# Two deformable convolutions on one core: the last unit's sampling products in two passes by rows of taps, and each pair's output finished in thirds on three engines

## The reference

```python
def gather(yi, xi): ...          # x at a whole pixel, 0 outside
val = gather(y0, x0) * (1-ly)*(1-lx) + gather(y0, x0+1) * (1-ly)*lx \
    + gather(y0+1, x0) * ly*(1-lx) + gather(y0+1, x0+1) * ly*lx      # per tap, at (y + ky - 1 + dy, x + kx - 1 + dx)
val = val * mask                                                     # second block only
out = einsum('bckhw,ock->bohw', val, w) + b
# block 1: x = x + out;  block 2: x = x + relu(norm1(out) * gamma + beta), norm1 over all of an image
```

## Time and profile before

| | us |
|---|---|
| median of 3 runs | 175.85 |
| lowest, highest | 174.75, 175.94 |
| execution profiled | 175.09 |
| its span in the profile | 173.2 |
| TensorE busy in it | 152.8 |
| ScalarE, VectorE busy | 108.3, 103.9 |

### The profile page before, as it was taken

How to read it: one execution, slowest core, us unless ns; L and a number is a source line. 1 busy time by engine, 2 the same in 40 slices (tenths; PEclk the granted TensorE clock), 3 DMA queues, 4 the chain that set the end, 5 groups by cost and what they waited for, 6 DMA issues and landing times.

```text
span 173.2 us, 4593 instructions
## 1 busy us (share of the span) xinstructions
PE 152.8 (88%) x1596; PEld 114.2 (66%) x1596; DVE 103.9 (60%) x244; ACT 108.3 (63%) x246; POOL 66.9 (39%) x129
## 2 busy tenths in 40 slices
PE   7998997989999989998798999998798989999820
PEld 2454643779897876986476876885566756888710
DVE  0333667987666565349976774449975747762042
ACT  3032769788778558369777566379787657863202
POOL 8511156544445425233344444234244516450010
PEclk9999999999999999999999999999999999999985
DMA  5986204400000000530000001510000000010001
GB/s 195 301 256 166 73 4 121 108 6 4 0 2 4 0 8 7 146 78 4 0 0 4 0 8 44 141 50 0 4 0 4 0 6 0 6 72 0 0 6 68
DMA packets 11988, 8.20 MB, mean 47 GB/s; under 512 B 3116, under 2 KB 10796, under 8 KB 11960
## 3 DMA queue, kind: packets, MB, share of 16 engines
q1 hardware_dynamic: 11672, 7.57, 15.4%
q10 hardware_dynamic: 288, 0.27, 0.5%
HBM read 3.31 MB, written 0.59 MB: 23 GB/s over the span
## 4 chain that ended last, share of the span: by engine, by line
PE 64%; issue 14%; DVE 14%; ACT 4%; POOL 1%; POOLq 0%; DVEq 0%; ACTq 0%
PE vb L929 16%; PE ob L945 14%; PE ring L899 8%; PE ring L891 8%; PE ob L855 8%; DVE s L719 4%; PE vb L1020 4%; DVE pos L665 2%; PE ring L843 2%; ACT xa L544 2%; DVE msk L672 2%; PE ring L874 1%; DVE ytent L711 1%; ACT off L495 1%; PE ring L884 1%
## 5 line engine op out<-in xcount | busy, mean ns | idle before, releaser
L452 POOL TENSOR_SCALAR xa<-xa 120x384 f32<-120x384 f32 x108 | 57.6, 540 | 72.1 <-ACT xa L544 71.6
L719 DVE SCALAR_TENSOR_TENSOR s<-xa,ring 120x384 f32<-120x384 f32 x108 | 58.0, 551 | 29.3 <-PE ring L891 26.1
L544 ACT ACTIVATE xa<-ring 120x384 f32<-120x384 f32 x108 | 51.0, 485 | 14.0 <-PE ring L899 13.3
L945 PE MATMUL ob<-val,w_d 128*64 128x192 f32 x432 | 42.9, 326 | 0.7 <-issue 0.7
L899 PE MATMUL ring<-pos,soon 68*64 68x384 f16 x216 | 37.7, 329 | 4.9 <-DVE s L719 2.7
L891 PE MATMUL ring<-ytent,soon 128*64 128x384 f16 x216 | 37.9, 328 | 0.8 <-DVE ytent L711 0.5
L945 PEld LDWEIGHTS ob<-val,w_d 128*64 128x64 f32 x432 | 34.4, 136 | 3.1 <-issue 1.7
L929 PE MATMUL vb<-s,shifted 120*64 120x216 f32 (+2 forms) x352 | 34.7, 315 | 0.4 <-ACT val L555 0.3
L929 PEld LDWEIGHTS vb<-s,shifted 120*64 120x64 f32 x352 | 24.1, 136 | 4.7 <-ACT val L555 1.1
L555 ACT ACTIVATE val<-vb 128x432 f32<-128x432 f32 x36 | 18.9, 525 | 8.2 <-PE vb L929 7.0
L899 PEld LDWEIGHTS ring<-pos,soon 68*64 68x64 f16 x216 | 14.7, 108 | 12.3 <-issue 7.4
(11 more groups left out here) (72 smaller groups left out, 113.2 us busy)
## 6 DMA issues: line engine op xcount, KB each, us to landing
shifted<-blk SPq DMA_DIRECT2D x8, 192.0 KB
shifted<-blk SPq DMA_DIRECT2D x8, 144.0 KB
shifted<-blk SPq DMA_DIRECT2D x8, 96.0 KB
soon<-c_soon SPq DMA_DIRECT2D x1, 640.0 KB, 6.5
x_l<-x SPq DMA_DIRECT2D x2, 288.0 KB, 4.3
w_o<-w_off SPq DMA_DIRECT2D x2, 288.0 KB, 4.0
w_d<-w_def SPq DMA_DIRECT2D x4, 144.0 KB, 3.8
late<-c_late SPq DMA_DIRECT2D x1, 576.0 KB, 6.1
```

The lines of the kernel that those rows point to most:

```text
L452: nc.gpsimd.tensor_scalar(v, v, 1.0, 0.0, ALU.min, ALU.max).then_inc(xu_ready, 1)
L544: nc.scalar.activation(xa[:, n % XA_BUFS, :], bank("x", n)[0:SPAN, 0:2 * UPX], ACT.Abs).then_inc(act_took, 1)
L719: nc.vector.scalar_tensor_tensor(out=s[u % 2][:, k // 3:k // 3 + 2 * THIRD, W * k:W * (k + 1)], in0=xa[:, n % XA_BUFS, :].rearrange("q (r ...
L945: last = mm(sums[64 * i:64 * i + 64, 0:UPX], w_d[l][:, t, 64 * i:64 * i + 64], val[u % 2][:, t // 3:t // 3 + THIRD, W * t:W * (t + 1)], st ...
```

## The change

**The last unit (u = 11).** Its windows are no longer 10, each with all its taps, but 17, cut by rows of taps: chunks 0 to 2 hold taps 0 to 5 (windows of 144 columns and two of 72), chunks 3 and 4 hold taps 6 to 8 (8 windows of 72). The columns in total are the same. Chunks 0 to 2 wait for DVE's product of tap 5 only, and stand among the last taps' fills and unit 10's weights; chunks 3 and 4 wait for tap 8. The weights of taps 0 to 5 wait for the values of chunk 2, those of taps 6 to 8 for chunk 4. ACT copies in 6 pieces instead of 5.

**The output.** ACT's ReLU covers two thirds of a pair (384 columns). DVE does the first third alone in two operations, then adds `x_mid` to the second; POOL adds it to the last. SP stores each third by its own DMA. Of the operations for scale and bias, -mean x gamma is now formed before the wait for rstd, and the two behind it do not depend on each other.

**Places.** The mean matmul of pair 0 stands behind a chunk of windows and two fills on TensorE. `x_mid` is read one place earlier on DVE for 4 units of the first layer, the offsets copy of stage 1 one place earlier on ACT, and the ReLU of pair 0 one place later.

```diff
+ROW = 3 * W
+LAST_CHUNKS = [((1, 0, 6), (2, 0, 6), (3, 0, 6)), ((4, 0, 6), (5, 0, 6), (6, 0, 6)), ((0, 0, 3), (7, 0, 6), (8, 3, 6)),
+               tuple((w, 6, 9) for w in range(2, 6)), tuple((w, 6, 9) for w in range(6, 10))]
+FIRST_ROWS = 3
+def evacuated(n):
+    u = min(n // CHUNKS, UNITS - 1)
+    c = n - CHUNKS * u
+    return 5 * u + (2 + c if u < UNITS - 1 else c + 1 + (c >= 2))
...
-    "sums": {"ACT": 14, "DVE": 19}, "summed": {"DVE": 20},
+    "sums": {"ACT": 13, "DVE": 18}, "summed": {"DVE": 20},
...
+LAST_UNIT = {
+    "windows": {"PE": (-11, -10, -8, -3, -2)}, "values": {"ACT": (-10, -9, -7, -2, -1)},
+    "weighted": {"PE": (-2, -2, -2, -1, -1, -1, 2, 2, 2)},
+}
...
-    "final mean": {"DVE": 1, "PE": 1}, "final var": {"DVE": 2, "PE": 2, "POOL": 2},
-    "final out": {"DVE": 15, "ACT": 11},
+    "final mean": {"DVE": 1, "PE": 2}, "final var": {"DVE": 2, "PE": 2, "POOL": 2},
+    "final out": {"DVE": 16, "ACT": 12, "POOL": 14},
...
             for p in range(PAIRS):
-                sp.wait_ge(res_ready, p + 1)
-                sp.dma_start(pair_of(out, p), res[:, p, :]).then_inc(stored, 16)
+                for j in range(2):
+                    sp.wait_ge(res_ready, 2 * p + j + 1)
+                    sp.dma_start(pair_of(out, p)[:, UPX * j:UPX * (j + 1)], res[:, p, UPX * j:UPX * (j + 1)]).then_inc(stored, 16)
+                sp.wait_ge(res_third, p + 1)
+                sp.dma_start(pair_of(out, p)[:, 2 * UPX:HW], res[:, p, 2 * UPX:HW]).then_inc(stored, 16)
...
+            def final_out(p):
+                c = slice(2 * UPX, HW)
+                pool.wait_ge(relu_ready, p + 1)
+                nc.gpsimd.tensor_tensor(res[:, p, c], res[:, p, c], x_mid[:, p, c], ALU.add).then_inc(res_third, 1)
...
+                if u == UNITS - 1:
+                    if c == 2:
+                        parts = [(d[:, 0:8:7, 0:ROW], 0), (d[:, 7:9, ROW:2 * ROW], 2 * ROW)]
+                    elif c < 2:
+                        parts = [(d[:, 3 * c + 1:3 * c + 4, 0:2 * ROW], 0)]
+                    else:
+                        parts = [(d[:, 4 * c - 10:4 * c - 6, 2 * ROW:SLOT], 0)]
...
             def final_out(p):
-                act.wait_ge(fin_ready, p + 1)
-                nc.scalar.activation(res[:, p, :], y[:, p, :], ACT.Relu, scale=fin[:, p, 6:7], bias=fin[:, p, 7:8])\
+                c = slice(UPX, HW)
+                act.wait_ge(fin_ready, 2 * p + 2)
+                nc.scalar.activation(res[:, p, c], y[:, p, c], ACT.Relu, scale=fin[:, p, 6:7], bias=fin[:, p, 7:8])\
...
+                then(nc.vector.tensor_scalar(fin[:, p, 3:4], fin[:, p, 2:3], gamma, -1.0, ALU.mult, ALU.mult))
                 dve.wait_ge(fin_rstd, p + 1)
-                then(nc.vector.tensor_scalar(fin[:, p, 6:7], fin[:, p, 5:6], gamma, None, ALU.mult))
-                then(nc.vector.tensor_tensor(fin[:, p, 4:5], fin[:, p, 2:3], fin[:, p, 6:7], ALU.mult))
-                nc.vector.tensor_scalar(fin[:, p, 7:8], fin[:, p, 4:5], -1.0, beta, ALU.mult, ALU.add).then_inc(fin_ready, 1)
+                nc.vector.tensor_scalar(fin[:, p, 6:7], fin[:, p, 5:6], gamma, None, ALU.mult).then_inc(fin_ready, 1)
+                nc.vector.tensor_scalar(fin[:, p, 7:8], fin[:, p, 3:4], fin[:, p, 5:6], beta, ALU.mult, ALU.add)\
+                    .then_inc(fin_ready, 1)
...
+                a, b = (slice(UPX * j, UPX * (j + 1)) for j in range(2))
+                dve.wait_ge(fin_ready, 2 * p + 2)
+                then(nc.vector.tensor_scalar(res[:, p, a], y[:, p, a], fin[:, p, 6:7], fin[:, p, 7:8], ALU.mult, ALU.add))
+                nc.vector.scalar_tensor_tensor(out=res[:, p, a], in0=res[:, p, a], scalar=0.0, in1=x_mid[:, p, a],
+                                               op0=ALU.max, op1=ALU.add).then_inc(res_ready, 1)
                 dve.wait_ge(relu_ready, p + 1)
-                nc.vector.tensor_tensor(res[:, p, :], res[:, p, :], x_mid[:, p, :], ALU.add).then_inc(res_ready, 1)
+                nc.vector.tensor_tensor(res[:, p, b], res[:, p, b], x_mid[:, p, b], ALU.add).then_inc(res_ready, 1)
...
+                by_rows = u == UNITS - 1
+                if by_rows:
+                    wait_taken(pe, "s", TAPS * u + (5 if c < FIRST_ROWS else 8))
+                elif c == 0:
                     wait_taken(pe, "s", TAPS * (u + 1) - 1)
...
-                    pe.wait_ge(val_ready, 5 * (u + 1))
+                    if u < UNITS - 1:
+                        pe.wait_ge(val_ready, 5 * (u + 1))
...
+                if u == UNITS - 1 and t in (0, 6):
+                    pe.wait_ge(val_ready, evacuated(CHUNKS * u + (4 if t else FIRST_ROWS - 1)))
```

More of the change, by code:

```diff
@@ L92 @@
 SECOND = {
-    "xt": {"PE": (-18, -16), "ACT": (-18, -15)}, "conv": {"PE": (-26, -25, -24, -23)}, "offsets": {"ACT": -6},
+    "xt": {"PE": (-18, -16), "ACT": (-18, -15)}, "conv": {"PE": (-26, -25, -24, -23)}, "offsets": {"ACT": -7},
     "parts": {"DVE": -4}, "split": {"ACT": (6, 8, 11, 13), "DVE": (-1, 0, 4, 6)}, "largest": {"DVE": -2},
@@ L134, in program @@
         for name in ("windows", "values", "weighted"):
-            put(base, name, u, UNIT)
+            put(base, name, u, UNIT if u < UNITS - 1 else LAST_UNIT)
         if engine == ("ACT" if m >= PAIRS else "DVE"):
@@ L334, in build @@
         fin_stats, fin_var, fin_rstd, fin_ready = sem("fin_stats"), sem("fin_var"), sem("fin_rstd"), sem("fin_ready")
-        relu_ready, res_ready, stored = sem("relu_ready"), sem("res_ready"), sem("stored")
+        relu_ready, res_ready, res_third, stored = sem("relu_ready"), sem("res_ready"), sem("res_third"), sem("stored")
         g_act, g_dve, g_pe, g_sum, g_out = ([sem(f"{n}{m}") for m in range(STAGES)]
@@ L421, in _ @@
             for p in range(PAIRS):
-                sp.wait_ge(res_ready, p + 1)
-                sp.dma_start(pair_of(out, p), res[:, p, :]).then_inc(stored, 16)
-            sp.wait_ge(stored, 16 * PAIRS)
+                for j in range(2):
[3 more added lines that the diff above has]
+                sp.dma_start(pair_of(out, p)[:, 2 * UPX:HW], res[:, p, 2 * UPX:HW]).then_inc(stored, 16)
+            sp.wait_ge(stored, 3 * 16 * PAIRS)
         @block.gpsimd
@@ L452, in clamp @@
                 nc.gpsimd.tensor_scalar(v, v, 1.0, 0.0, ALU.min, ALU.max).then_inc(xu_ready, 1)
-            part = {"x": clamp, "norm": norm, "final var": final_var}
+            def final_out(p):
+                c = slice(2 * UPX, HW)
+                pool.wait_ge(relu_ready, p + 1)
+                nc.gpsimd.tensor_tensor(res[:, p, c], res[:, p, c], x_mid[:, p, c], ALU.add).then_inc(res_third, 1)
+            part = {"x": clamp, "norm": norm, "final var": final_var, "final out": final_out}
             pool.wait_ge(cleared, 1)
@@ L551, in values @@
                     act.wait_ge(sums_full, u - 1)
+                d = val[u % 2]
+                if u == UNITS - 1:
[5 more added lines that the diff above has]
+                        parts = [(d[:, 4 * c - 10:4 * c - 6, 2 * ROW:SLOT], 0)]
+                    for to, at in parts:
+                        w, size = to.shape[1], to.shape[2]
+                        nc.scalar.activation(to, vb[:, n % 2, at:at + w * size].rearrange("p (w c) -> p w c", w=w), ACT.Copy)\
+                            .then_inc(val_ready, 1)
+                    return
                 v = vb[:, n % 2, 0:2 * SLOT].rearrange("p (w c) -> p w c", w=2)
-                d = val[u % 2]
                 if c:
@@ L919, in windows @@
                     shifted_wait(pe, m)
+                by_rows = u == UNITS - 1
+                if by_rows:
+                    wait_taken(pe, "s", TAPS * u + (5 if c < FIRST_ROWS else 8))
+                elif c == 0:
                     wait_taken(pe, "s", TAPS * (u + 1) - 1)
                 if n >= 2:
-                    before = n - 2
-                    pe.wait_ge(val_ready, 5 * (before // CHUNKS) + 2 + before % CHUNKS)
-                for w in CHUNK_WINDOWS[c]:
+                    pe.wait_ge(val_ready, evacuated(n - 2))
+                to = 0
+                for w, a, b in LAST_CHUNKS[c] if by_rows else [(w, *taps_of(w)) for w in CHUNK_WINDOWS[c]]:
+                    if not by_rows:
+                        to = SLOT * (w % 2) + W * a
                     at, r = divmod(first(THIRD * j - 1 + w), ROWS)
-                    a, b = taps_of(w)
                     x_t = shifted[m % 2][:, at, r - 1, :] if r else blk[m % 2][:, at, :]
                     for i in range(2):
-                        last = mm(vb[64 * i:64 * i + 64, n % 2, SLOT * (w % 2) + W * a:SLOT * (w % 2) + W * b],
+                        last = mm(vb[64 * i:64 * i + 64, n % 2, to:to + W * (b - a)],
                                   x_t[:, 64 * i:64 * i + 64], s[u % 2][:, THIRD * i + w, W * a:W * b],
                                   start=True, stop=True)
+                    to += W * (b - a)
                 last.then_inc(vb_full, 1)
```

## The result

The changed kernel took 174.44 us (median of 19 runs, 172.84 to 174.89) against 175.62 for the kernel before (19 runs beside it): ratio 0.9934 [0.9914, 0.9954], or 1.2 us less, inside the 1% that was to count as no change. The forecast was 173.3, from a sum of 2.2 us. The time lies outside the forecast's own range (172.3 to 174.2) and inside the one with the rivals (172.0 to 175.0). The gain is real, and about half of what was forecast. The execution profiled took 174.29 us, its span 172.4 against 173.2.

A forecast was written before the change was run, and what follows sets the result against it. TensorE was taken to bound the kernel up to the last output row, then the tail's chain. 0.48 + 0.40 + 0.46 + 0.85 = 2.2 us off 175.09 gives 172.9, off median 175.85, 173.65; forecast 173.3, range 172.3 to 174.2.

The forecast's parts named there:

- Step 1: Pair 0's mean and variance on TensorE: mean behind a chunk and two fills, new variance wait 0.7; gain 0.48 us.
- step 2: Ring banks behind pair 0's variance: DVE's s products come sooner, so 0.4 of 0.6 us of TensorE waits goes.
- step 3: Last unit: one 0.90 us wait before chunk 0 replaces waits of 1.31, later waits covered; gain 0.46 us.
- step 4: Tail from rstd on: shorter scale-and-bias chain, ReLU of 384, output in thirds with POOL's add 0.7; gain 0.85 us.
- pair 0's finishing: Three shorter DVE operations instead of one of 1.10, a POOL add and two more SP DMAs: costed at nothing.
- A: Rival, 15%: the mid-run gain does not reach the end, ytent's ACT-DVE chain or DVE's products set the pace; 174.1 us.
- B: Rival, 12%: weight loads bind the short windows of chunks 3 and 4, 1.2 us lost; 174.4 us.
- C: Rival, 12%: POOL's add over 1 us and small pieces slow as large, 0.8 of the tail's gain lost; 174.1 us.
- D: Rival, 5%: the clock drops at the new idle of 0.90 before chunk 0; about 180 us.

The follow-up runs named there:

- e1: Kernel before with only the last unit's two passes by rows of taps: 174.95 us against 175.44, ratio 0.9964.
- e4: Kernel before with only x_mid read one s product earlier (four units) and stage 1's offsets copy one xa earlier: 175.68 us, ratio 1.0014.
- e2: Kernel before with only the output in thirds and the shorter scale-and-bias chain: 174.81 us, ratio 0.9987.
- e3: Kernel before with only pair 0's mean matmul moved behind a chunk and two fills: 174.87 us, ratio 0.9959.
- e10: Changed kernel with the edits of e6 and e8 together: 173.10 us, ratio 0.9833 to the kernel before.
- e5: Changed kernel with pair 0's variance matmul two places later, behind a chunk and two fills: 173.76 us.
- e7: Changed kernel with unit 9's last values copy on ACT behind one xa copy instead of ahead of it: 174.52 us.
- e11: Changed kernel with the edits of e6, e8 and e7 together: 172.46 us, ratio 0.9782 to the kernel before.
- e12: Changed kernel with the edits of e6, e8, e7 and e5 together: 172.56 us, ratio 0.9830 to the kernel before.
- e6: Changed kernel with unit 10's first weights ahead of chunk 0 in the last unit: 173.86 us.
- e8: Changed kernel with POOL out of the output, DVE adding the last 384 columns in one operation and SP storing two pieces: 173.10 us.
- e9: The changed kernel measured again, no edit: 174.16 us against 175.72 for the kernel before, ratio 0.9893.

## Where the prediction was right and where it failed

Of the 2.19 us of the sum the structure gave 1.32. Step 1 fell short by 0.11, step 2 by its whole 0.40, step 3 by 0.22 and step 4 by 0.41, and 0.27 came that nobody had booked. Step 2 had the wrong engine; in steps 3 and 4 the mechanism was right and terms were mis-sized. The forecast of 173.3 lay a little below what the sum gives off the kernel before's 175.62 (173.4), since half of it went by the faster execution profiled.

**Step 1, right in mechanism, 0.37 for 0.48.** Mean behind the fills, variance 1.02 behind it, as said. The mean started 1.18 after the fill ahead was issued (139.06 to 140.24) and not the 1.07 of chunk and fills: TensorE's way from a fill to this matmul is 0.29 from start to start (139.95 to 140.24) where I had counted 0.17. The kernel before had shown it, 140.85 to 141.11 in front of the variance.

**Step 2, wrong, 0 for 0.40.** This is the step that failed. I saw two waits for ring banks beside DVE's late s products and gave them to DVE. DVE did come sooner, as forecast, and the wait that was DVE's went: from x fill to s fill there are 0.42 before and in e1 and e4, 0.28 in e2, 0.19 in e3 and 0.17 in the changed kernel. Nothing followed, since the second wait took it all: variance to mask fill stayed 3.43 (3.42 in e10) in every kernel but e5, e7, e11 and e12. e7 shows that ACT frees the mask's bank, by a changed order of ACT alone. A bank is freed by the engine that takes its last fill, and the mask's had held an x fill, which ACT takes; its `xa` starts 2.80 behind the variance in both kernels. The earlier trace rows show no releaser for these waits ("issue"), and I did not ask for ACT's timeline.

**A gain not forecast, 0.27**, from the mask fill to the tap 5 fill. It is the term that the prediction put at nothing under "pair 0's finishing": e2 has 0.22 of it alone, where the s fill no longer waits for the product behind DVE's add of 1.10. Mask fill to tap 5 fill is 8.80 in e2, 8.94 or 8.95 in e1, e3 and e4, and 9.01 before. The rest, 0.05 or 0.06, also lies between executions of the same code (8.74 in the changed kernel, 8.80 in e6). Whether it is the place of DVE's output operations or their length that counts, no run separates.

**Step 3, right in mechanism, 0.24 for 0.46.** All covers held: no wait is recorded behind chunk 0, and chunks 3 and 4 took 0.5 each. The wait was 1.10 for 0.90. DVE started 0.46 after the fill (forecast 0.47) and took 0.55, ending at 154.44, but TensorE's matmul starts at 154.70: 0.26 from DVE's end, of which I had counted 0.05. All six profiles of this order (the changed kernel, e1, e5, e7, e8, e9) have the same wait, so it is not chance; why it is longer than the 0.05 from bn_aggr to the mean matmul, no run tells. And the place was poor: with unit 10's weights in front (e6) the same split gives 1.14.

**Step 4, 0.44 for 0.85.** Scale and bias: 1.09 to the ReLU against 1.06 forecast. ReLU of 384 columns 0.71, not 0.64. POOL's add 0.76, not 0.7, and started 1.87 behind rstd, not 1.78; SP's last store at 2.74 behind rstd instead of 2.51. The data and the end took 2.13 after it, forecast 2.10. And 0.15 was lost in front of bn_aggr, which idles 0.18 behind bn_stats in every kernel with this part (y copy to bn_aggr 0.85 in the four without it and about 1.00 in the others); why, no run tells. The Trainium skill, GPSIMD Engine Reference, section 3.1, gives by my estimate 0.42 for the add's elements beside a fixed part; 0.59 agrees with that and 0.76 does not contradict it. Pair 0's add took 0.59 while DVE idled, and the last one 0.76 with DVE adding, in all six profiles with POOL's third. That points to the neighbour, but no run has the last add without it.

**The rivals.** A (the gain does not reach the end): refuted as put, since 0.37 arrived whole; but its kind, another engine than the one named sets the pace, is what ate step 2. B (weight loads bind): refuted, 32 records of 0.031 in 1.00 us with a load of 64 columns each. The Trainium skill, TensorE: Matmul & The Clock Gate, section LDWEIGHTS, has 53 ns for such a load, an estimate of 1.7 us for 32 in a row; the trace does not bear it out as a spacing. C (the tail gives little): its conditions did not come, with POOL's add at 0.76 and not over 1, but 0.41 of its 0.8 was missing. D (the clock drops at chunk 0's wait): it did not in any profile. The length of a wait did not tell where it would drop: the changed kernel's dip at 28.8 has no TensorE wait over 0.49 in the 8 us before it, while the kernel before waited 1.18 at 164.8 and kept its clock until 167.5.

## What to carry to other kernels

A wait that stands beside a late engine is not yet that engine's: find which operation frees the very buffer, and what stands ahead of it on its own queue, before a gain is booked. Where a new dependence is made, take the time from one engine's end to the next one's start from a row of the same kind (here 0.05 from bn_aggr to a matmul and 0.26 from an s product to a matmul), and place work that is ready in front of the piece that waits. A long operation that gates nothing itself can still stand ahead of one that does, so cost its place as well as its length. A third engine for the last piece has to pay for its seam and its own pace; here two pieces on two engines beat three on three by 0.21 in e8's profile.

## What the hardware showed

- Two executions of nearly the same code differed in clock by place: half speed from 28.8 to 32.2 us in one and full speed in the other, and 1.5 to 2.0 us lie between the runs at a mean granted clock of 0.99 and of 0.98 (e9).
- An add of 192 columns on POOL: 0.59 with DVE idle, 0.76 beside an add on DVE; DVE did 384 columns in 0.56.
- From the end of a DVE product of 384 columns to the start of the TensorE matmul that needed it: 0.26; from the end of bn_aggr to its matmul: 0.05.
- 32 matmul records of 72 columns, each with its own load of 64 columns: 1.00 us.
